# Reordering the last routing stage of an attention and mixture kernel around its first expert tiles

## What is computed

```python
x = x + attn(layernorm(x))                      # 8 batches, 512 tokens, width 512
z = layernorm(x)
weights = z @ W_r + b_r
sel = weights > topk(weights, 128).values[-1]
h = gelu(z[selected] @ W1 + b1)                 # width 2048
blk = h @ W2 + b2
x = x + where(sel, blk * weights, z)
```

## Time and profile before

| | |
|---|---|
| median of 3 runs | 2390.52 us (2385.95 to 2391.7) |
| the profiled execution: its time | 2390.49 us |
| its span, first to last instruction | 2388.7 us |
| PE busy / DVE / ACT / POOL | 97% / 77% / 62% / 68% |
| granted TensorE clock, mean | 0.992 |
| the chain that ended last, share on PE | 67% |
| last chunk of batch 7 ends | 2184.95 us |
| last expert product ends | 2379.16 us |

### The profile page before, as it was taken

The page is one execution under the profiler, slowest core; times in us unless marked ns, Lnnn a source line. Parts: engine busy times, 40 slices in busy tenths (PEclk is TensorE's granted clock), DMA queues, the critical chain, the costliest instruction groups (busy, mean ns, idle before and its releaser), DMA issues.

```text
span 2388.7 us, 42080 instructions
## 1 busy us (share of the span) xinstructions
PE 2313.6 (97%) x13200; PEld 2034.8 (85%) x13200; DVE 1836.8 (77%) x6087; ACT 1489.5 (62%) x4165; POOL 1632.8 (68%) x1267
## 2 busy tenths in 40 slices
PE   6999999999999999999999999999998999998998
PEld 5799899989888898999899898989887788886787
DVE  8589898988888898989898888888883665566311
ACT  6577777777777777777777777777773111212343
POOL 2677877787787778777877877787883444444554
PEclk9999999999999999999999999999999999999999
DMA  5222222222222223223222322222333444453332
GB/s 172 74 59 62 73 76 58 72 73 67 54 80 69 61 60 84 65 58 81 67 65 58 87 59 67 63 72 60 124 89 123 162 170 154 152 197 102 109 116 79
DMA packets 143602, 213.34 MB, mean 89 GB/s; under 512 B 15009, under 2 KB 53281, under 8 KB 143393
## 3 DMA queue, kind: packets, MB, share of 16 engines
q1 hardware_dynamic: 137248, 196.17, 27.8%
q10 hardware_dynamic: 4224, 8.39, 0.9%
q0 software_dynamic: 1920, 6.24, 0.8%
HBM read 90.47 MB, written 53.22 MB: 60 GB/s over the span
## 4 chain that ended last, share of the span: by engine, by line
PE 67%; DVE 11%; POOL 9%; ACT 5%; DMA 3%; issue 2%; SPq 0%; POOLq 0%; ACTq 0%; DVEq 0%
PE bank L641 19%; PE bank L1116 13%; PE bank L654 10%; PE bank L684 7%; PE bank L721 7%; PE bank L698 4%; DMA s_swap<-s_full 3%; PE bank L1677 3%; PE bank L1658 3%; POOL s_full L591 2%; POOL s_swap L592 2%; POOL s_full L595 2%; DVE bank L884 1%; DVE shift L880 1%; DVE pt_lo L894 1%
## 5 line engine op out<-in xcount | busy, mean ns | idle before, releaser
L591 POOL TENSOR_TENSOR s_full<-s_full,rope 128x512 f32<-128x512 f32 x256 | 336.5, 1314 | 334.9 <-DMA s_swap<-s_full 334.5
L595 POOL TENSOR_TENSOR s_full<-s_full,s_swap 128x512 f32<-128x512 f32 x256 | 330.7, 1292 | 37.6 <-POOL s_swap L592 0.9
L592 POOL TENSOR_TENSOR s_swap<-s_swap,rope 128x512 f32<-128x512 f32 x256 | 330.7, 1292 | 0.0
L599 POOL TENSOR_TENSOR qk_lo<-s_full,qk_hi 128x512 fp32r<-128x512 f32 x256 | 326.2, 1294 | 0.1
L768 ACT ACTIVATE pt_hi<-bank 128x384 fp32r<-128x384 f32 (+1 forms) x384 | 174.5, 528 | 229.1 <-PE bank L698 229.0
L654 PE MATMUL bank<-wv_hi,xt_hi 128*128 128x256 f32 x1024 | 300.1, 293 | 0.0
L774 ACT ACTIVATE bank<-bank,shift 128x512 f32<-128x512 f32 (+3 forms) x512 | 256.9, 502 | 60.1 <-DVE bank L884 59.8
L1100 POOL TENSOR_TENSOR o_lo<-o_raw,o_hi 128x2048 fp32r<-128x2048 f32 x31 | 142.3, 4591 | 217.6 <-ACT o_hi L1276 185.9
L654 PE MATMUL bank<-wv_hi,xt_lo 128*128 128x256 f32 x1024 | 289.7, 283 | 0.0
L654 PE MATMUL bank<-wv_lo,xt_hi 128*128 128x256 f32 x1024 | 289.7, 283 | 0.0
L884 DVE TENSOR_REDUCE bank<-bank 128x8 f32<-128x512 f32 (+3 forms) x512 | 253.1, 494 | 0.0
(11 more groups left out here) (189 smaller groups left out, 6899.0 us busy)
## 6 DMA issues: line engine op xcount, KB each, us to landing
s_swap<-s_full SPq DMA_DIRECT2D x512, 128.0 KB, 2.3
o_scratch<-s_swap SPq DMA_DIRECT2D x128, 256.0 KB, 2.0
o_raw<-o_scratch SPq DMA_DIRECT2D x32, 1024.0 KB, 5.4
w_raw<-in_L_ffn_W SPq DMA_DIRECT2D x64, 256.0 KB, 2.9
xin<-in_L_attn_x SPq DMA_DIRECT2D x14, 1024.0 KB, 5.6
z_scratch<-z ACTq DMA_DIRECT2D x8, 1024.0 KB, 4.3
out<-x SPq DMA_DIRECT2D x32, 256.0 KB, 2.1
wq_raw<-in_L_attn_Wq SPq DMA_DIRECT2D x16, 256.0 KB, 3.1
```

What stands on the lines that cost most here:

```text
L591: nc.gpsimd.tensor_tensor(s_full[k][:], s_full[k][:], rope[:, 0, :], ALU.mult).then_inc(cos_done[k], 1)
L592: nc.gpsimd.tensor_tensor(s_swap[k][:], s_swap[k][:], rope[:, 1, :], ALU.mult).then_inc(sin_done[k], 1)
L595: nc.gpsimd.tensor_tensor(s_full[k][:], s_full[k][:], s_swap[k][:], ALU.add).then_inc(roped[k], 1)
L599: nc.gpsimd.tensor_tensor(qk_lo[k][:], s_full[k][:], f32(qk_hi[k][:]), ALU.subtract).then_inc(lo_done[k], 1)
```

## The change

It has six parts.

1. POOL makes `o_lo` of a chunk in four instructions of 128x512 values instead of one of 128x2048. This holds for 31 of the 32 chunks.
2. PE does `hidden(0)` ahead of the last chunk (b = 7, k = 3), in the body of batch 6, and `hidden(1)` behind that chunk, ahead of the wait for the residual sums. Behind the ones matmul there is now the product of tile 2 and one more hidden layer, and so on: product and hidden layer of the last body are regrouped.
3. ACT does gelu of tiles 0 and 1 ahead of the square root, without the high parts of the weights of tiles 3 and 4 between; these come behind the square root and behind the store of z. Gelu of tile 2 comes ahead of that store.
4. DVE clears `rows` and makes `hid_lo` of tile 0 ahead of the residual sums of the last batch; tile 1's low part takes the place of tile 0's, tile 2's comes between the second and the third score sum, tile 3's ahead of the counts, tile 4's behind the one-hot rows.
5. In the last body DVE does the four "keep" instructions (L1473) behind the one-hot rows.
6. POOL's `fetch(0)` to `fetch(3)` and `fetch(4)` to `fetch(7)` come one tile later.

```diff
     def low(self, pool, b, k):
         pool.wait_ge(self.hi_split, b * self.K + k + 1)
-        self.nc.gpsimd.tensor_tensor(self.o_lo[k % 2][:], self.o_raw[k % 2][:], f32(self.o_hi[k % 2][:]),
-                                     ALU.subtract).then_inc(self.lo_split, 1)
+        for g in range(self.G):
+            last = self.nc.gpsimd.tensor_tensor(self.o_lo[k % 2][:, g], self.o_raw[k % 2][:, g], f32(self.o_hi[k % 2][:, g]), ALU.subtract)
+        last.then_inc(self.lo_split, 1)
...
                     first(0)
+                    first(1)
                 act.wait_ge(step, b * NS + 9)
                 nc.scalar.activation(sd[:], ve[:], ACT.Sqrt).then_inc(sd_ready, 1)
+                if not more:
+                    weights_high(3)
                 if not begun(b):
                     z_high(act, b - 1)
+                if not more:
+                    first(2)
...
                 else:
+                    hidden(1)
                     pe.wait_ge(x1_ready, B * T + 1)
-                    first(0)
+                    product(0)
                     turn_rows(pe, b - 1)
-                    first(1)
-                    first(2)
+                    hidden(2)
+                    product(1)
+                    hidden(3)
...
                 else:
-                    first(3)
-                    first(4)
+                    product(2)
+                    hidden(4)
...
                 else:
-                    first(5)
+                    product(3)
+                    hidden(5)
...
+                if more == "next":
+                    pe.wait_ge(zsel_lo_done, B // 2)
+                    hidden(0)
                 if more:
                     chunk(b + 1, 3)
+                else:
+                    product(4)
...
+                if not more:
+                    clear()
+                    dve.wait_ge(lo_split, B * K)
+                    first(0)
                 dve.wait_ge(x_loaded, b * 16 + 16)
...
                 for t in range(T):
+                    if not more and t == 2:
+                        first(2)
                     dve.wait_ge(z2_ready, b * T + t + 1)
...
+        def clear():
+            wait_split_free(dve)
+            nc.vector.memset(rows[:], 0.0).then_inc(rows_cleared, 1)
```

More of the change, by code:

```diff
@@ L1297, in body @@
                 else:
-                    for f in range(1, EARLY):
+                    weights_high(4)
+                    for f in range(3, EARLY):
                         first(f)
@@ L1305, in _ @@
             attend_scalar(act)
-            first, rest = ex_scalar(act)
+            first, weights_high, rest = ex_scalar(act)
             high(1, 0)
@@ L1372, in body @@
                 last.then_inc(info_ready, 1)
+                if more == "next":
+                    pe.wait_ge(zsel_lo_done, B // 2)
+                    hidden(0)
                 if more:
                     chunk(b + 1, 3)
+                else:
+                    product(4)
             attend_tensor(pe)
-            first, rest = ex_tensor(pe)
+            hidden, product, rest = ex_tensor(pe)
             batches(pe, body)
@@ L1468, in body, with keep @@
                 v.tensor_tensor(selcum[:, 3:4], selcum[:, 2:3], sel[:, 2:3], ALU.add).then_inc(sel_ready, 1)
[L1469 to L1476, removed]
+                def keep():
+                    for t in range(T):
+                        v.scalar_tensor_tensor(out=x1[:, t], in0=z2[:, t], scalar=unsel[:, t:t + 1], in1=x1[:, t],
+                                               op0=ALU.mult, op1=ALU.add).then_inc(x1_kept, 1)
+                if more:
+                    keep()
                 dve.wait_ge(slot_ready, b + 1)
@@ L1483, in body @@
                 if not more:
+                    first(4)
+                    keep()
                     first(5)
@@ L1628, in body @@
             nc.scalar.activation(hid_hi[s][:], hid[s][:], ACT.Copy).then_inc(hid_hi_done, 1)
-            if n + 2 < NT:
+            if ahead and n + 2 < NT:
                 high(n + 2)
@@ L1641, in first @@
             else:
-                body(n)
+                body(n, ahead=n not in (1, 2))
         def rest():
@@ L1646, in rest @@
                 tiles(g, body)
-        return first, rest
+        return first, high, rest
     def tensor(pe):
@@ L1683, in step @@
                 turn_rows(pe, B - 1)
-        def first(n):
-            if n == 0:
-                pe.wait_ge(zsel_lo_done, GB)
-                hidden(0)
-            step(n)
         def rest():
             for g in range(NG):
-                tiles(g, step)
-        return first, rest
+                tiles(g, step, begun=EARLY - 1)
+        return hidden, product, rest
     def vector(dve):
@@ L1727, in rest @@
                 final(GB + q)
-        return low, rest
+        return low, clear, rest
     return sync, gpsimd, scalar, tensor, vector
```

23 lines of the change are left out of this document (11 added, 12 removed).

## The result

The changed kernel takes 2376.99 us (median of 6 runs, 2374.43 to 2379.61), the kernel before beside it 2390.72 (2385.95 to 2392.08, 6 runs): ratio 0.9941, 95% interval 0.9931 to 0.9951. That is 13.7 us between the medians, 14.1 by the ratio, or 0.6% faster; 2375 was predicted. The profiled execution of the changed kernel took 2374.43 us with a span of 2372.6, 16.1 us less than the span of 2388.7 before; 15.6 were predicted for it. This execution is the fastest of its six, while that of the kernel before is at its median.

What follows compares the result with a forecast made beforehand. TensorE was taken to bound the loop, with 12.2 us of gaps behind the last chunk. 2390.49 - 19.6 (gaps, waits, low clock) + 3.9 left over + 0.1 = 2374.9, told as 2375 us; range 2367 to 2382.

Steps and rivals of the forecast that it cites:

- Batch 6, 3.8 us: At batch 6's ones matmul: diag gets in between o_lo's pieces, winning the 2.0 us wait and its low clock, 3.8 us.
- Batch 0, 0.4 us: In batch 0: six DVE instructions meet four o_lo pieces and are done 0.4 us earlier; bounds -0.5 and 3.5.
- The last batch, 15.8 less 3.9 = 11.9 us: Behind t, the last chunk's end: 15.8 us of gaps and low clock to win, 3.9 left over, bounds 0 and 6.4.
- +3.5 by four pieces: Last batch's DVE chain to diag: low parts of tiles 3 and 4, four POOL pieces, add 3.5 us, to t + 17.2.
- The split, 5.1 us a chunk in the loop: On POOL: four o_lo pieces take about 5.1 us against 4.59 for one instruction, covered in the loop.
- slower rival: In the loop: pieces colliding with DVE exceed 9.0 us a chunk and TensorE waits; at 10.1 us, 2398 us; chance 0.03.
- The table load: At the last batch's square root: a 1.28 us load without the page's 1.38 us drain, which would make the sum 1.4 worse.
- Tile 9's `w_lo` wait closes: In the last batch: earlier stores of the last rows and fetches one tile later close the 1.8 us w_lo wait.
- DVE does not get in: In batches 0 and 6: diag waits for all o_lo pieces, 5.1 us; 2380 us; chance 0.13.
- everything fits: Last batch's two chains miss each other, left over 0 to 0.5, and batch 0's diag gets through; 2368 us; chance 0.18.
- the early low part holds the sums: Last batch on DVE: tile 0's low part, 13 us late, starts the residual sums 9 us late; some 2384; chance 0.07.
- A new wait further on: Last batch: left over at its upper bound, 2.5 more, and tile 9's 3.7 us stay; 2381 us; chance 0.12.

Runs made afterwards that it cites:

- e6: The changed kernel with the last batch's square root ahead of gelu 1 on ScalarE and tile 1's hid_lo behind z on DVE; 2374.16 us, ratio 0.9935.
- e12: The changed kernel with the clearing of rows back behind the last batch; 2375.64 us.
- e7: The changed kernel with product 2 ahead of the last ones matmul, and products 3 and hidden 5 moved up one place behind it; 2375.01 us.
- e2: The kernel before with o_lo in four pieces and nothing else; 2384.27 us, ratio 0.9964.

## Why the prediction was right

The number held: 2375 against 2377, 15.6 us against 16.1 in the profiled executions. By kind of time it was close too: for waits it had 12.2 + 2.0 + 0.4 - 3.0 = 11.6 us where idle time fell by 10.3, for low clock 3.6 + 1.8 - 0.9 = 4.5 where it was 4.4, and 1.2 us of shorter groups it did not have. Place by place there are two errors, too little for batch 0 and too much for the last batch, and that they cancel is luck.

- **Batch 6, 3.8 us.** Measured 3.79 between these two profiles. But 2.2 of it belong to the wait and to the split; the other 1.6 are low clock that fell there in one execution and not in the next. And the way is another than I had it: `diag` ends before the next `o_lo` starts, not between its pieces.
- **Batch 0, 0.4 us.** Measured 2.15: 0.56 from the split, by the count I made (one instruction per boundary; `diag` took 4.98 us through four pieces), the rest low clock. Its wait is 1.8 us instead of 2.3. The prediction's terms left out that the 48 matmuls behind it took 11.55 us in the first profile. The `o_lo` wait grew by 0.4 us (0.5 predicted); it does not show in the first mark, since attention ended 0.6 us earlier in that execution (the `o_lo` that is waited for begins at 1825.71 against 1826.31).
- **The last batch, 15.8 less 3.9 = 11.9 us.** Measured 9.96. The gaps and the slow groups of before all went. (Left over are 4.4 us of wait and 2.4 of low clock, 6.8 in all; the forecast had 3.9, upper bound 6.4.) TensorE came at t + 14.2 as counted, and the bare chain is t + 13.6 as counted. The term that failed is the contention: "+3.5 by four pieces" was 5.0, by five: tile 5's first piece came ahead of `wcol`, since it waits for no product. So the wait was 4.4 (3.0 predicted, upper bound 4.6), and behind it low clock came in full: 0.94 + 1.49 where I had put half of 1.8. All five executions with a wait of 4.4 us had it, 1.6 to 2.7 us of it.
- **The split, 5.1 us a chunk in the loop.** Measured 5.02, and no gap in the loop. The slower rival, 9.0 us a chunk, was far off.
- **The table load.** In the changed kernel:

```profile
2185.63 1.28 ACT L1286 ACT_TABLE_LOAD   x1
2186.93 0.21 ACT L1286 ACTIVATE sd<-ve 128x4 f32<-128x4 f32 x1
```

0.02 us lie between load and square root, as in the earlier trace rows. The rule in the Trainium skill, page "ScalarE: Activation LUTs", What ACT_TABLE_LOAD costs, of a drain of some 1.38 us beside each load, would have put `diag` at t + 18.6. That is where it was, but for another reason: with the low parts away and the same table loads it is at t + 13.6. A sum that comes out right doesn't show which term made it so.
- **Tile 9's `w_lo` wait closes.** It did; but neither the fetch one tile later nor the clearing is needed for it: each can be undone, and the split alone, with both in their old places, has no such wait. The stores of the last rows begin 13 us earlier (2219.0 against 2232.3; 17 were predicted) and may be it; that was not tried by itself, and in the split alone the stores are late too (2229.1). It stays open.

Of the rivals, "DVE does not get in" and "everything fits" fell, and so did "the early low part holds the sums": it ended at 2178.6, 3.0 us before the last sum began. "A new wait further on" was right in its first half, what was left over; it went past the upper bound.

Not taken apart are parts 2 and 5 of the change, and parts 3 and 4 only in pieces (`e6` has gelu of tile 1 behind the square root again, `e12` the clearing in its old place, and neither brings a wait for `hid_lo`). That these waits close because tile 0 is ready under the chunk is read from the rows, not shown by a run.

## What to carry to other kernels

Before you sum terms of two profiles, measure the same program twice between marks inside it: here the loop's length repeats to 0.01 us while the start of the stage wanders by 8 us, and 3.2 us of low clock change place. When one engine's pieces hold up another's instructions, count each piece of the one as one stopped instruction of the other, at a full piece's length, and look for a place where nobody waits before cutting it smaller: moving four low parts behind `diag` gave 5.2 us (3.1 of wait, the rest low clock), cutting `o_lo` in four gave 3.0 and cutting it in two as much.

## What the hardware showed that I had not expected

- A GpSimd piece of 128x512 (1.26 to 1.30 us alone) held one VectorE instruction that read SBUF, however small: 128x4 operations took 1.1 to 1.3 us instead of 0.17. The counts, which read a PSUM bank, were not held. The pieces themselves grow far less: the pair of tile 4 took 3.01 us instead of 2.53.
- The engine's clock after a wait is no fixed price: the waits of 1.8 to 2.4 us at batches 0 and 6 were followed by full clock in 15 of 17 cases, and the two exceptions are in one execution; waits of 4.4 us were always followed by low clock, 1.6 to 2.7 us of it in five executions, and so were others in the last batch: one of 2.1 us (1.84 and 3.67, `e6`), one of 2.7 (`e7`), those of 2.4 and 2.1 in `e2`, but not its wait of 1.9. Ahead of the first mark, the `o_lo` wait of 2.1 to 2.5 us was followed by low clock in nine of the 13 profiles that have it. So the count at batches 0 and 6 is good for those places only.
- The clearing (3.47 us on VectorE) slowed the gather of rows from 1.11 to 3.00 us when the gather began 2.0 us behind it (before, and `e2`), and not at all when it began 0.4 us behind it (the changed kernel) or together with it (`e12`). Why the later one suffers was not tried. The prediction's rule, a gather locked out for the whole of a VectorE instruction, is not borne out for this clearing: the two gathers of 1.11 us began within it. Whether the clearing runs in a two-port mode, which that rule asks for, no run shows.
